# A transformer block with ALiBi attention: first norm before the weights' biases, diagonal bias added by 64-column matmuls

## The chip, the core and the metric

One NeuronCore of one Trainium2 chip runs one program: a recurrent mixer, a feed-forward layer, an attention layer, and the same feed-forward layer again. The metric is the device time of one execution in microseconds, the median of three runs. The change touches the attention layer alone.

## The reference, cut to what matters

Shapes: x is 8 × 1024 × 256 (batch, tokens, channels), 16 heads of 16 channels, all in float32.

```python
def _L0_attn_b_ref(x, Wqkv, bqkv, Wout, bout):
    qkv = (x @ Wqkv + bqkv).reshape(B, L, 3, n_heads, head_dim)
    q, k, v = (qkv[:, :, 0], qkv[:, :, 1], qkv[:, :, 2])
    scores = jnp.einsum('bqhd,bkhd->bhqk', q, k) / math.sqrt(head_dim)
    bias = -jnp.abs(pos[None, :] - pos[:, None])
    scores = scores + slopes[None, :, None, None] * bias[None, None]
    probs = jax.nn.softmax(scores, axis=-1)
    out = jnp.einsum('bhqk,bkhd->bqhd', probs, v).reshape(B, L, D)
    return out @ Wout + bout

x = x + attn_a(layernorm(x)); x = x + ffn(layernorm(x))
x = x + _L0_attn_b_ref(_layernorm(x), ...); x = x + ffn(layernorm(x))
```

The term `slopes * -|q - k|` is the one that the diagonal blocks of the change belong to.

## The kernel before, in words

**Tiling.** `attention` works through 32 groups g (8 batches × 4 groups of 4 heads). Queries and keys of a head lie in "stacks" of 64 rows (`q_stack`, `k_stack`): 48 rows of q and k split into a high and a low part, 14 rows that carry the ALiBi bias as products, and 2 rows with the row maxima as a shift. Two heads stand above one another in the 128 partitions, so a score matmul uses one half of TensorE's rows (rows 0 to 63, or 64 to 127), and two of them can run side by side.

**Two score passes.** `find_maxima` makes scores with queries in the partitions (L1588: stationary q, moving 512 keys), and VectorE takes the row maxima from PSUM (L1807). The maxima go through DRAM into the shift rows. `attend` makes the scores again with keys in the partitions (L1649: stationary k, moving 512 queries), ScalarE takes exp of two heads at once (L1758, 1024 columns), and `weigh` multiplies with v (L1604, 128×17 stationary, 256 columns, accumulated in one PSUM bank, which ScalarE copies out at L1727).

**Diagonal blocks.** Bias rows cannot express |q - k| inside a 128×128 block on the diagonal: they have one sign there. `add_block_bias` (L1532) adds what is missing to the 128 columns of that block, with two bf16 matmuls (parts): stationary is `halves[rows, part]`, a 64×128 slice of the identity, moving is `tables[rows, ..., variant, part]`, 64×128. Each part fills half of the output's partitions and adds zeros to the other half. A score tile of 512 columns has such a block when its key half and its query half are the same ("here").

**Steps.** A step here is one value of (t, pair): two L1649 (one for each half of the rows), two row turns of `find_maxima` for a group ahead (two L1588), the blocks that either has, and eight records of L1604. There are 32 × 2 × 8 × 2 = 1024 such steps. Column scores have a block in 512 of them. Row turns alternate between a pair with a block and one without. The lead before the first step does 80 of the 2048 row turns, with the second stack and the first batch's values beside them.

**Order.** Every engine runs the same generators in the same order (`schedule`, `side_by_side`): for each g the steps, with the projections of a later group (`make_stacks`), a batch's values and its norm spread between. PSUM: two pairs of banks for column scores, one for the weighed values, three in a ring (`misc`) for everything else, the row turns included.

**Start of the layer.** SyncE issues in order: identity, x of batch 0, w_out, b_v, b_qk, scale_qk, b_out, w_qk, w_v, x of batch 1. GpSimd issues the casting loads: k_bias (to DRAM), the constant rows of both stacks, halves, tables. All loads from SyncE but x and the identity count on one semaphore, `weights_in`. VectorE waits for the whole count, widens b_v (L1848) and scales b_qk (L1849); TensorE makes b_v·Wout (L1667, L1668); VectorE adds it to b_out (L1851). ScalarE and GpSimd wait for that (`bias_made`) before the schedule begins. Only then comes the norm of batch 0: stats (L1778) on VectorE, L1861 to L1872 on GpSimd, transposes (L1546), then the first projection, whose high and low parts SyncE copies into the stacks by 28 small DMAs, then the first row turn.

## Time and profile before

| | us |
|---|---|
| median of three runs | 3480.31 (3478.15 to 3480.33) |
| the profiled execution | 3481.96 |
| its span, first to last instruction | 3480.2 |
| attention's start: first load issued to first row turn | 1157.4 to 1224.5 |
| lead: first row turn to first L1649 | 1224.5 to 1291.9 |
| steps: first to last L1649 | 1291.9 to 3098.2 |

```profile
PE 3223.5 (93%) x31396; PEld 1914.4 (55%) x31396; DVE 2473.6 (71%) x4742; ACT 1998.0 (57%) x2999; POOL 768.7 (22%) x888
PE   7999999967999389999999999999999999978998
PEclk8999999978999669999999999999999999999999
```

The first line is each engine's busy time over the whole span, PE being TensorE's matmuls and PEld its weight loads. The other two are the span in 40 equal slices of 87 us: PE's busy share in tenths, and the granted TensorE clock in tenths of full speed. The layer begins at the slice with the 3; its steps are the run of nines with a clock of 9 (which stands for 90% or more) behind it. A matmul's record covers its way through the array too, so records overlap, and a busy PE is no measure of how many columns it takes in.

### The profile page before, as it was taken

The page shows a single profiled execution, that of the slowest core. Times are in us where ns is not written, and L with a number is a line of the kernel's source. Part 1 is how long each engine was busy: PE and PEld are TensorE (multiplying, and loading weights), DVE is VectorE, ACT ScalarE, POOL GpSimd, SP SyncE. Part 2 cuts the span into 40 slices and gives each one's busy share as a digit, 9 for nine tenths or more (in the row PEclk, how much of TensorE's full clock was granted, in tenths as well). Part 3 has the DMA queues.
Part 4 walks back from the last instruction along what each step waited for, and adds up shares of the span by engine and source line. Part 5 has one row for each costly group of instructions (what it writes and reads, how often), then busy time and mean ns, then how long its engine had stood idle before and what let it go on. Part 6 is the DMA issues. An engine that isn't in the chain of part 4 may idle for free. (4 is left out here: it accounts for less than half of the span.)

```text
span 3480.2 us, 77977 instructions
## 1 busy us (share of the span) xinstructions
PE 3223.5 (93%) x31396; PEld 1914.4 (55%) x31396; DVE 2473.6 (71%) x4742; ACT 1998.0 (57%) x2999; POOL 768.7 (22%) x888
## 2 busy tenths in 40 slices
PE   7999999967999389999999999999999999978998
PEld 3666666655777244444444444444444444437777
DVE  6777777737777168767778677677786776817776
ACT  3444444524555117666667666666676666765555
POOL 3445444422222201011020020110201201011222
PEclk8999999978999669999999999999999999999999
DMA  1000000012111412121222131212221312111110
GB/s 51 14 26 27 26 26 26 14 49 70 49 49 43 92 34 44 27 53 36 44 47 44 23 68 29 57 31 43 47 45 24 68 30 49 24 41 61 55 54 33
DMA packets 110295, 145.49 MB, mean 42 GB/s; under 512 B 21616, under 2 KB 94208, under 8 KB 109152
## 3 DMA queue, kind: packets, MB, share of 16 engines
q1 hardware_dynamic: 109168, 137.69, 16.8%
q8 instruction: 249, 4.08, 0.5%
q0 software_dynamic: 768, 2.82, 0.4%
q14 instruction: 110, 0.90, 0.1%
HBM read 53.89 MB, written 38.24 MB: 26 GB/s over the span
## 5 line engine op out<-in xcount | busy, mean ns | idle before, releaser
L1807 DVE TENSOR_REDUCE b_half_max<-banks 128x1 f32<-128x512 f32 x2048 | 1314.3, 685 | 441.4 <-PE banks L1532 263.1
L1758 ACT ACTIVATE b_p_t<-banks 128x1024 f32<-128x1024 f32 x1024 | 1045.8, 1024 | 398.2 <-PE banks L1532 256.6
L1588 PE MATMUL banks<-b_k_stack,b_q_stack 62*128 62x512 f32 x2048 | 826.4, 475 | 34.6 <-issue 17.8
L1649 PE MATMUL banks<-b_q_stack,b_k_stack 64*128 64x512 f32 x2048 | 851.6, 469 | 0.0
L1604 PE MATMUL banks<-b_p_t,b_v 128*17 128x256 f32 x8192 | 640.9, 385 | 25.1 <-ACT b_pv L1727 24.5
L1649 PEld LDWEIGHTS banks<-b_q_stack,b_k_stack 64*128 64x128 f32 x2048 | 342.9, 185 | 432.3 <-issue 416.8
L1532 PE MATMUL banks<-b_tables,b_halves 64*128 64x128 bf16 x4096 | 435.8, 223 | 0.0
L1588 PEld LDWEIGHTS banks<-b_k_stack,b_q_stack 62*128 62x128 f32 x2048 | 336.4, 187 | 67.9 <-issue 24.6
L1137 ACT ACTIVATE ffn_relu<-banks,ffn_scale_fc 128x512 f32<-128x512 f32 x256 | 176.0, 687 | 234.2 <-PE banks L1069 234.2
L1082 PE MATMUL banks<-ffn_proj_t,ffn_r_hi 128*128 128x256 f32 x1024 | 262.0, 289 | 8.8 <-DVE ffn_r_lo L1263 8.8
L1604 PEld LDWEIGHTS banks<-b_p_t,b_v 128*17 128x17 f32 x8192 | 135.9, 95 | 225.3 <-issue 77.3
L1083 PE MATMUL banks<-ffn_proj_t,ffn_r_lo 128*128 128x256 f32 x1024 | 253.2, 280 | 0.0
L1532 PEld LDWEIGHTS banks<-b_tables,b_halves 64*128 64x128 bf16 x4096 | 185.0, 96 | 117.1 <-issue 57.3
L1261 DVE CAST ffn_r_hi<-ffn_square 128x512 fp32r<-128x512 f32 x256 | 128.8, 503 | 142.3 <-ACT ffn_square L1141 140.8
L1889 POOL TENSOR_TENSOR b_qk_lo<-b_qk,b_qk_hi 128x512 fp32r<-128x512 f32 x64 | 81.7, 1276 | 655.4 <-ACT b_qk L1707 498.0
L1082 PEld LDWEIGHTS banks<-ffn_proj_t,ffn_r_hi 128*128 128x128 f32 x1024 | 194.4, 190 | 24.3 <-DVE ffn_r_lo L1263 14.9
L1065 PE MATMUL banks<-ffn_x_hi,ffn_fc_t 128*128 128x512 f32 x512 | 203.4, 397 | 0.0
L1066 PE MATMUL banks<-ffn_x_lo,ffn_fc_t 128*128 128x512 f32 x512 | 202.9, 396 | 0.0
L1083 PEld LDWEIGHTS banks<-ffn_proj_t,ffn_r_lo 128*128 128x128 f32 x1024 | 193.4, 189 | 8.2
L1319 POOL TENSOR_TENSOR ffn_x<-ffn_x,ffn_scaled_out 128x256 f32<-128x256 f32 x128 | 107.9, 843 | 402.6 <-DVE ffn_scaled_out L1274 402.6
L1263 DVE TENSOR_TENSOR ffn_r_lo<-ffn_square,ffn_r_hi 128x512 fp32r<-128x512 f32 x256 | 177.2, 692 | 8.8
L1141 ACT ACTIVATE ffn_square<-ffn_relu 128x512 f32<-128x512 f32 x256 | 161.8, 632 | 8.1
(232 smaller groups left out, 4728.1 us busy)
## 6 DMA issues: line engine op xcount, KB each, us to landing
ffn_x<-x SPq DMA_DIRECT2D x32, 512.0 KB, 3.8
b_q_stack<-b_qk_hi SPq DMA_DIRECT2D x256, 64.0 KB
b_k_stack<-b_qk_hi SPq DMA_DIRECT2D x256, 64.0 KB
a_x<-hidden_states SPq DMA_DIRECT2D x16, 512.0 KB, 4.3
x<-a_x SPq DMA_DIRECT2D x16, 512.0 KB, 2.9
x<-ffn_x SPq DMA_DIRECT2D x16, 512.0 KB, 2.8
b_x<-x SPq DMA_DIRECT2D x8, 1024.0 KB, 6.2
b_k_stack<-b_qk_lo SPq DMA_DIRECT2D x128, 64.0 KB
```

Of the source, the lines that this page charges most:

```text
L1065: pe.matmul(b, fc_t[:, kt, cols], x_hi[:, kt, :], start=kt == 0, stop=False)
L1066: pe.matmul(b, fc_t[:, kt, cols], x_lo[:, kt, :], start=False, stop=False)
L1082: pe.matmul(b[:, 0:DIM], r_hi[par][:, m, i * P:(i + 1) * P], proj_t[:, m, :], start=m == 0, stop=False)
L1083: last = pe.matmul(b[:, 0:DIM], r_lo[par][:, m, i * P:(i + 1) * P], proj_t[:, m, :], start=False, stop=m == HT - 1)
L1137: act.activation(relu[use % 2][:, :], high[use % 3], ACT.Relu, scale=scale_fc[:, m:m + 1]).then_inc(relu_made, 1)
L1263: dve.tensor_tensor(r_lo[par][:, m, :], square[use % 2][:, :], r_hi[par][:, m, :].bitcast(F32), ALU.subtract).then_inc(r_lo_made, 1)
L1532: last = pe.matmul(out, halves[rows, part, :], tables[rows, g % GROUPS * PAIRS + pair, variant, part, :], start=False, stop=part == PARTS ...
L1588: last = pe.matmul(m, q_stack[rows, slot, qb * P:(qb + 1) * P], k_stack[rows, slot, half * BANK:(half + 1) * BANK], start=True, stop=not h ...
L1604: last = pe.matmul(values[i * SLOT:i * SLOT + VW, cols], v[:, kb, hg * GROUP + i, :], p_t[(2 * t + i % 2) % P_BUFS][:, i // 2, cols], star ...
L1649: last = pe.matmul(out, k_stack[stack, slot, kb * P:(kb + 1) * P], q_stack[stack, slot, half * BANK:(half + 1) * BANK], start=True, stop=n ...
L1758: act.activation(p_t[use % P_BUFS][:, :, :], scores[use % 2], ACT.Exp, scale=slopes()[pair][0]).then_inc(p_made, 1)
L1807: dve.tensor_reduce(half_max[:, (pair + rg * PAIRS) * QB + qb, half:half + 1], misc.at["max", g, turn], axis=AX.X, op=ALU.max, negate=True ...
```

## The change

The identity becomes one 64×64 unit matrix for each half of the partitions (`unit`), and it is the moving operand; the table is stationary, taken with the other `variant`, since it now comes out transposed. Each part writes 64 of the block's 128 columns, in all 128 partitions. The number of matmuls and of weight loads stays.

At the start, the weights count on three semaphores (qk, v, out), and w_qk is loaded first. Nothing waits for all of them: b_qk is scaled behind the first stats, b_v is widened with the first values, b_v·Wout is made by TensorE behind the eighth tile of the first values, and GpSimd waits for the sum at its first use. GpSimd's loads wait until x of batch 0 has landed; unit and tables are issued behind the seventh and eighth normalized tile.

```diff
--- before.py
+++ after.py
@@ -82,7 +82,7 @@
     by_head = power[:, :, :, None, None] * short
     c["c_block"] = by_head.reshape(GROUPS, ROWGROUPS, GROUP // ROWGROUPS, 2, P // STACK, STACK, P).transpose(
         1, 5, 0, 2, 3, 4, 6).reshape(P, HEADS // ROWGROUPS, 2, P // STACK, P)
-    c["c_halves"] = np.tile(np.eye(P).reshape(P // STACK, STACK, P).transpose(1, 0, 2), (ROWGROUPS, 1, 1))
+    c["c_unit"] = np.tile(np.eye(STACK), (ROWGROUPS, 1))
@@ -1392,7 +1392,7 @@
         PARTS = P // STACK
         WIDTH = BANK // 2
 
-        ident, halves = sb("ident", [P, P]), sb("halves", [P, PARTS, P], BF16)
+        ident, unit = sb("ident", [P, P]), sb("unit", [P, STACK], BF16)
         tables = sb("tables", [P, HEADS // ROWGROUPS, 2, PARTS, P], BF16)
@@ -1427,7 +1427,8 @@
 
 
         x_in_sem, x_out_sem = [sem(f"x_in{i}") for i in range(X_BUFS)], [sem(f"x_out{i}") for i in range(X_BUFS)]
-        ident_in, weights_in, bias_cast, tables_cast = sem("ident_in"), sem("weights_in"), sem("bias_cast"), sem("tables_cast")
+        ident_in, qk_weights_in, v_weights_in, out_weights_in = sem("ident_in"), sem("qk_weights_in"), sem("v_weights_in"), sem("out_weights_in")
+        bias_cast, tables_cast, scaled = sem("bias_cast"), sem("tables_cast"), sem("scaled")
         half_set, cleared, widened = sem("half_set"), sem("cleared"), sem("widened")
         bias_ready, bias_made = sem("bias_ready"), sem("bias_made")
@@ -1446,7 +1447,7 @@
         att_turned, att_t_made = sem("att_turned"), sem("att_t_made")
         y_ready, y_made, y_added, y_biased = sem("y_ready"), sem("y_made"), sem("y_added"), sem("y_biased")
 
-        WEIGHTS, TABLES = 5 + GROUPS + KT, 2 * ROWGROUPS + 2
+        QK_WEIGHTS, OUT_WEIGHTS, TABLES = GROUPS + 2, KT + 2, 2 * ROWGROUPS + 2
         misc = Ring([banks[:, i, :] for i in (5, 6, 7)], (cleared, 1))
         STEPS, STACKS, VALUES, NORMALIZE = GROUP * HALVES * QB, 2, QB, 1 + QB
 
@@ -1527,9 +1528,11 @@
 
         def tensor(pe):
             def add_block_bias(out, g, pair, rg, variant):
+
                 rows = slice(rg * STACK, (rg + 1) * STACK)
                 for part in range(PARTS):
-                    last = pe.matmul(out, halves[rows, part, :], tables[rows, g % GROUPS * PAIRS + pair, variant, part, :],
+                    cols = slice(part * STACK, (part + 1) * STACK)
+                    last = pe.matmul(out[:, cols], tables[rows, g % GROUPS * PAIRS + pair, 1 - variant, part, :], unit[rows, :],
                                      start=False, stop=part == PARTS - 1, tile_position=(rg * STACK, 0))
                 return last
 
@@ -1547,19 +1550,34 @@
                     last.then_inc(xn_turned, 1)
                     yield
 
+            def bias_of_values():
+
+                m, (used, n) = misc.take(("bias",), (bias_made, 1))
+                pe.wait_ge(used, n)
+                pe.wait_ge(out_weights_in, 16 * OUT_WEIGHTS)
+                pe.wait_ge(widened, 1)
+                pe.matmul(m[:, 0:DIM], b_v_wide[:, 0, :], w_out[:, 0, :], start=True, stop=False)
+                pe.matmul(m[:, 0:DIM], b_v_wide[:, 1, :], w_out[:, 1, :], start=False, stop=True).then_inc(bias_ready, 1)
+
             def make_values(b):
                 xn_t = xn_ts[b % 2]
+                if b == 0:
+                    pe.wait_ge(v_weights_in, 16)
                 pe.wait_ge(xn_t_made, 4 * (b + 1))
                 for i in range(QB):
                     m, (used, n) = misc.take(("v", b, i), (v_made, QB * b + i + 1))
                     pe.wait_ge(used, n)
                     pe.matmul(m[:, 0:DIM], xn_t[:, 0, i * P:(i + 1) * P], w_v[:, 0, :], start=True, stop=False)
                     pe.matmul(m[:, 0:DIM], xn_t[:, 1, i * P:(i + 1) * P], w_v[:, 1, :], start=False, stop=True).then_inc(v_ready, 1)
+                    if (b, i) == (0, QB - 1):
+                        bias_of_values()
                     yield
 
             def make_stacks(g):
                 b, hg = divmod(g, GROUPS)
                 xn_t = xn_ts[b % 2]
+                if g == 0:
+                    pe.wait_ge(qk_weights_in, 16 * QK_WEIGHTS)
                 pe.wait_ge(xn_t_made, 4 * (b + 1))
                 for half in range(HALVES):
                     cols = slice(half * BANK, (half + 1) * BANK)
@@ -1661,11 +1679,6 @@
             follow, finish_tails = tails(weigh, conclude)
             pe.wait_ge(ident_in, 16)
             pe.wait_ge(cleared, 1)
-            pe.wait_ge(weights_in, 16 * WEIGHTS)
-            m, _ = misc.take(("bias",), (bias_made, 1))
-            pe.wait_ge(widened, 1)
-            pe.matmul(m[:, 0:DIM], b_v_wide[:, 0, :], w_out[:, 0, :], start=True, stop=False)
-            pe.matmul(m[:, 0:DIM], b_v_wide[:, 1, :], w_out[:, 1, :], start=False, stop=True).then_inc(bias_ready, 1)
             schedule(attend, find_maxima, make_stacks, make_values, normalize, row_parts=2)
             finish_tails()
 
@@ -1698,6 +1711,8 @@
                     use, cols = 2 * g + half, slice(half * BANK, (half + 1) * BANK)
                     m = misc.at["qk", g, half]
                     act.wait_ge(qk_ready, use + 1)
+                    if use == 0:
+                        act.wait_ge(scaled, 1)
                     if g:
                         for i in range(GROUP):
                             act.wait_ge(stacked[slot_of(g - 1) + i], 112 * ((g - 1) // SETS + 1))
@@ -1764,7 +1779,6 @@
             follow, finish_tails = tails(weigh, conclude)
             act.wait_ge(ident_in, 16)
             act.wait_ge(cleared, 1)
-            act.wait_ge(bias_made, 1)
             schedule(attend, find_maxima, make_stacks, make_values, normalize)
             finish_tails()
 
@@ -1781,11 +1795,20 @@
                 for i in range(QB):
                     last = dve.bn_aggr(mean_var[:, i, :], stats[:, i, :])
                 last.then_inc(moments, 1)
+                if b == 0:
+                    dve.wait_ge(qk_weights_in, 16 * QK_WEIGHTS)
+                    dve.tensor_scalar(b_scaled[:, :], b_qk[:, :], scale_qk[:, 0:1], None, ALU.mult).then_inc(scaled, 1)
                 for _ in range(NORMALIZE):
                     yield
 
             def make_values(b):
-                for _ in range(VALUES):
+                if b == 0:
+                    dve.wait_ge(out_weights_in, 16 * OUT_WEIGHTS)
+                    dve.tensor_copy(b_v_wide[:, :, :], spread(b_v[:, :], P)).then_inc(widened, 1)
+                for i in range(VALUES):
+                    if (b, i) == (0, VALUES - 1):
+                        dve.wait_ge(bias_ready, 1)
+                        dve.tensor_tensor(b_out[:, :], b_out[:, :], misc.at["bias",][:, 0:DIM], ALU.add).then_inc(bias_made, 1)
                     yield
 
             def make_stacks(g):
@@ -1844,11 +1867,6 @@
             dve.memset(values, 0.0).then_inc(cleared, 1)
             dve.wait_ge(ident_in, 16)
             dve.wait_ge(cleared, 1)
-            dve.wait_ge(weights_in, 16 * WEIGHTS)
-            dve.tensor_copy(b_v_wide[:, :, :], spread(b_v[:, :], P)).then_inc(widened, 1)
-            dve.tensor_scalar(b_scaled[:, :], b_qk[:, :], scale_qk[:, 0:1], None, ALU.mult)
-            dve.wait_ge(bias_ready, 1)
-            dve.tensor_tensor(b_out[:, :], b_out[:, :], misc.at["bias",][:, 0:DIM], ALU.add).then_inc(bias_made, 1)
             schedule(attend, find_maxima, make_stacks, make_values, normalize)
             finish_tails()
 
@@ -1871,6 +1889,9 @@
                     for j in range(2):
                         pool.tensor_scalar(xn[j][:, :], x[:, i + j, :], minus_mean[:, i + j:i + j + 1], norm_rstd[:, i + j:i + j + 1],
                                            ALU.add, ALU.mult).then_inc(xn_made, 1)
+                    if (b, i) == (0, QB - 2):
+                        pool.dma_start(unit[:, :], d["c_unit"]).then_inc(tables_cast, 16)
+                        pool.dma_start(tables[:, :, :, :, :], d["c_block"]).then_inc(tables_cast, 16)
                     yield
                     yield
 
@@ -1911,6 +1932,8 @@
                     pool.wait_ge(y_made, tile + 1)
                     pool.tensor_tensor(x, x, y[tile % 2][:, :], ALU.add).then_inc(y_added, 1)
                     pool.wait_ge(y_added, tile + 1)
+                    if tile == 0:
+                        pool.wait_ge(bias_made, 1)
                     pool.tensor_tensor(x, x, b_out[:, :], ALU.add).then_inc(y_biased, 1)
                     yield
 
@@ -1924,14 +1947,12 @@
             follow, finish_tails = tails(weigh, conclude)
             pool.memset(minus_half[:, :], -0.5).then_inc(half_set, 1)
             every_slot = lambda ap: ap.unsqueeze(1).to_broadcast([ap.shape[0], SETS * PAIRS, SEQ])
+            pool.wait_ge(x_in_sem[0], 16)
             pool.dma_start(k_bias, d["c_kbias"]).then_inc(bias_cast, 16)
             for first in range(0, P, STACK):
                 pool.dma_start(q_stack[first + MAIN:first + SHIFTROW, :, :], every_slot(d["c_qrows"])).then_inc(tables_cast, 16)
                 pool.dma_start(k_stack[first + SHIFTROW:first + STACK, :, :], every_slot(d["c_krows"])).then_inc(tables_cast, 16)
-            pool.dma_start(halves[:, :, :], d["c_halves"]).then_inc(tables_cast, 16)
-            pool.dma_start(tables[:, :, :, :, :], d["c_block"]).then_inc(tables_cast, 16)
             pool.wait_ge(half_set, 1)
-            pool.wait_ge(bias_made, 1)
             schedule(attend, find_maxima, make_stacks, make_values, normalize)
             finish_tails()
 
@@ -2010,15 +2031,15 @@
             follow, finish_tails = tails(weigh, conclude)
             sp.dma_start(ident[:, :], d["c_ident"]).then_inc(ident_in, 16)
             load(0)
-            sp.dma_start(w_out[:, :, :], tiled(d["Wout"])).then_inc(weights_in, 16)
+            sp.dma_start(w_qk[:, :, :, :].rearrange("p k g n -> p k (g n)"), tiled(d["Wqkv"][:, 0:2 * DIM])).then_inc(qk_weights_in, 16)
+            sp.dma_start(scale_qk[:, :], d["c_qkscale"]).then_inc(qk_weights_in, 16)
+            for g in range(GROUPS):
+                sp.dma_start(b_qk[:, g:g + 1], column(d["bqkv"][g * P:(g + 1) * P])).then_inc(qk_weights_in, 16)
+            sp.dma_start(w_v[:, :, :], tiled(d["Wqkv"][:, 2 * DIM:3 * DIM])).then_inc(v_weights_in, 16)
+            sp.dma_start(w_out[:, :, :], tiled(d["Wout"])).then_inc(out_weights_in, 16)
             for kt in range(KT):
-                sp.dma_start(b_v[:, kt:kt + 1], column(d["bqkv"][2 * DIM + kt * P:2 * DIM + (kt + 1) * P])).then_inc(weights_in, 16)
-            for g in range(GROUPS):
-                sp.dma_start(b_qk[:, g:g + 1], column(d["bqkv"][g * P:(g + 1) * P])).then_inc(weights_in, 16)
-            sp.dma_start(scale_qk[:, :], d["c_qkscale"]).then_inc(weights_in, 16)
-            sp.dma_start(b_out[:, :], d["bout"].partition_broadcast(P)).then_inc(weights_in, 16)
-            sp.dma_start(w_qk[:, :, :, :].rearrange("p k g n -> p k (g n)"), tiled(d["Wqkv"][:, 0:2 * DIM])).then_inc(weights_in, 16)
-            sp.dma_start(w_v[:, :, :], tiled(d["Wqkv"][:, 2 * DIM:3 * DIM])).then_inc(weights_in, 16)
+                sp.dma_start(b_v[:, kt:kt + 1], column(d["bqkv"][2 * DIM + kt * P:2 * DIM + (kt + 1) * P])).then_inc(out_weights_in, 16)
+            sp.dma_start(b_out[:, :], d["bout"].partition_broadcast(P)).then_inc(out_weights_in, 16)
             load(1)
             schedule(attend, find_maxima, make_stacks, make_values, normalize)
             finish_tails()
```

## Rows read from the trace of the kernel before

**Rows 1.** Costliest groups (xcount | busy, mean ns of one | idle before, releaser)

```profile
L1807 DVE TENSOR_REDUCE b_half_max<-banks 128x1 f32<-128x512 f32 x2048 | 1314.3, 685 | 441.4 <-PE banks L1532 263.1
L1532 PE MATMUL banks<-b_tables,b_halves 64*128 64x128 bf16 x4096 | 435.8, 223 | 0.0
```

**Rows 2.** Three stretches: length, busy us of each engine, then PEclk, DMA share, GB/s

```profile
1157.00:1224.40 67.40, 12.96 (x28) 5.92 (x28) 4.93 (x22) 5.28 (x8) 13.37 (x21) 0.53 0.55 113
1224.40:1292.00 67.60, 62.88 (x203) 31.49 (x203) 48.54 (x80) 6.42 (x14) 2.98 (x3) 0.65 0.19 34
1310.00:3103.00 1793.00, 1744.11 (x17287) 851.01 (x17284) 1321.90 (x2223) 1225.35 (x1455) 216.28 (x279) 1.00 0.21 40
```

**Rows 3.** Timeline of TensorE, two steps: start us, us, what

```profile
1600.78 0.50 PE L1649 MATMUL banks<-b_q_stack,b_k_stack 64*128 64x512 f32 x1
...
1602.01 0.50 PE L1649 MATMUL banks<-b_q_stack,b_k_stack 64*128 64x512 f32 x1
...
1602.35 0.28 PE L1532 MATMUL banks<-b_tables,b_halves 64*128 64x128 bf16 x2
...
1603.40 0.50 PE L1649 MATMUL banks<-b_q_stack,b_k_stack 64*128 64x512 f32 x1
```

**Rows 4.** The same view, two steps with blocks in the column scores

```profile
1623.16 0.50 PE L1649 MATMUL banks<-b_q_stack,b_k_stack 64*128 64x512 f32 x1
...
1624.56 0.50 PE L1649 MATMUL banks<-b_q_stack,b_k_stack 64*128 64x512 f32 x1
...
1624.90 0.29 PE L1532 MATMUL banks<-b_tables,b_halves 64*128 64x128 bf16 x4
...
1625.31 0.29 PE L1532 MATMUL banks<-b_tables,b_halves 64*128 64x128 bf16 x4
1625.54 0.63 PE L1604 MATMUL banks<-b_p_t,b_v 128*17 128x256 f32 x8
1626.09 0.50 PE L1649 MATMUL banks<-b_q_stack,b_k_stack 64*128 64x512 f32 x1
```

**Rows 5.** Timeline of the weight loads in the step at 1602.01

```profile
1602.34 0.11 PEld L1532 LDWEIGHTS banks<-b_tables,b_halves 64*128 64x128 bf16 x2
1602.41 0.19 PEld L1649 LDWEIGHTS banks<-b_q_stack,b_k_stack 64*128 64x128 f32 x1
```

**Rows 6.** Matmuls of the mixer with 64 and 32 moving columns, by form

```profile
L341 PE MATMUL banks<-a_q_up,a_k_up 32*64 32x32 f32 x4480 | 83.9, 217 | 0.0
L341 PE MATMUL banks<-a_q,a_k 32*64 32x64 f32 x896 | 38.9, 244 | 0.0
```

**Rows 7.** Waits, 1292 to 3103: us in total, times, longest

```profile
PEld banks L1604 <- ACT b_pv L1727: 37.7, 63, 1.0
```

**Rows 8.** Timeline of all engines at the layer's start

```profile
1157.80 0.60 SPq L1944 DMA_DIRECT2D b_x<-x  x1
1157.92 0.80 POOL L1927 DMA_DIRECT2D b_k_bias<-c_kbias  x1 [0.42 <-issue]
...
1160.99 0.61 POOL L1931 DMA_DIRECT2D b_halves<-c_halves  x1
...
1183.15 0.29 DVE L1848 COPY b_b_v_wide<-b_b_v 128x256 f32<-128x256 f32 x1 [24.59 <-DMA b_w_v<-Wqkv]
...
1186.01 2.71 DVE L1778 BATCH_NORM_STATS2 b_stats<-b_x 128x6 f32<-128x256 f32 x8
...
1189.60 0.25 POOL L1861 TENSOR_SCALAR b_norm_rstd<-b_mean_var 128x8 f32<-128x8 f32 x1 [27.44 <-DVE b_mean_var L1782]
...
1224.47 0.89 PE L1588 MATMUL banks<-b_k_stack,b_q_stack 62*128 62x512 f32 x2 [17.82 <-issue]
```

**Rows 9.** Loads issued in 1157 to 1170: KB each, median us to landing

```profile
b_x<-x SPq DMA_DIRECT2D x1, 1024.0 KB, 16.5
...
b_tables<-c_block POOLq DMA_DIRECT2D x1, 1024.0 KB, 18.5
b_k_bias<-c_kbias POOLq DMA_DIRECT2D x1, 896.0 KB, 7.7
```

**Rows 10.** Landing of x, all eight batches

```profile
DMA to landing us min/median/max: 4.4/5.6/16.5
```

## The prediction

> **What bounds the kernel now.** I first read the costliest groups. The row maxima on VectorE cost 1314 us and the diagonal matmuls 436 us of records, so both could bound the layer [rows 1]. The stretches decide it: while the steps run (1310 to 3103), PE is busy 97% at full clock, VectorE 74%, ScalarE 68% [rows 2]. Records overlap, so I then read the timeline of TensorE, step by step, and there the bound is plain. A step without blocks takes 1.23 us from one L1649 to the next, one with blocks in the row turns 1.39 us [rows 3], one with blocks in the column scores 1.40 us, and one with both 1.53 us [rows 4]. The same work always takes the same time, so these steps wait for no other engine; the blocks cost 0.17 us alone and 0.30 together. The start has another bound: from 1157.8 to 1183.15 the engines wait for loads, then b_v·Wout takes until 1186.0, and only there does the norm begin [rows 8]. The lead (67.6 us) has 80 reductions in 48.5 us of VectorE beside 62.9 us of PE at mean clock 0.65: the two take turns [rows 2].
>
> **Part 1: diagonal matmuls of 64 columns.** Number of matmuls and loads: unchanged. Per matmul: 128 columns at the granted full clock of 2.4 GHz are 53 ns, 64 are 27, so at most 27 ns go. How much of it is on the path?
> - In a row-turn step, the order on one half of the array is: scores, part 0, part 1, load of the next stationary (L1649), its 512 columns. That load starts at 1602.41, 0.07 us after the blocks' first load, that is as part 1 starts, and takes 0.19 [rows 5]; part 1's columns run beside it. So only part 0 stands on the path: 27 ns. The step's second block lies on the other half, whose scores were already under way; it ends before the scores of the first half do. It costs nothing now and gives nothing.
> - A column-score step is the mirror of it: 27 ns.
> - In a step with both, both halves have a block twice. The first pair (1624.90) again gives part 0 only. The second pair (1625.31) is the last thing before L1604 at 1625.54 [rows 4], with no load to hide in; there both parts count, 54 ns. Together 81 ns.
>
> Counts: column blocks are in 512 of 1024 steps; row turns made during steps are 2048 − 80 = 1968, so 984 pairs, 492 with a block, half of these (246) beside a column block. That is 246 with both, 246 with row blocks only, 266 with column blocks only: 246 × 81 + 512 × 27 ns = 19.9 + 13.8 = 33.7 us. The lead comes below. Taken off: in 63 steps the first L1604 of a new sum waits for ScalarE's copy L1727 (37.7 us in all, 0.6 each) [rows 7]; that chain starts at the L1604 before, so what TensorE does meanwhile is covered. I take 45 ns a step as lost, 63 × 45 ns = 2.8 us. Part 1 gives 31 us.
>
> Bounds: no row shows a bf16 matmul of 64 columns. Nearest are the mixer's records, 244 ns with 64 fp32 columns and 217 with 32, 27 ns apart [rows 6]: a narrower moving operand does shorten a matmul at this size. The pair of diagonal loads lasts 0.11 us where one lasts about 0.10 [rows 5], so loads can follow one another some 15 ns apart, less than 27. From above: if all four or eight 27 ns of a step counted, 246 × 216 + 512 × 108 ns = 108 us; the layout of the step rules most of this out, and I take 36 us as upper end. From below: 0, if something other than columns sets the pace. I stay at 31, nearest to the step rows. VectorE does not take over: after the change the mean step is (1.23 + 1.36 + 1.37 + 1.45)/4 = 1.35 us with two reductions, whose starts can lie 0.61 us apart (48.5 us for 80), 1.21 us. Exp is one of 1.02 us a step.
>
> The Trainium skill speaks against this part: "TensorE: Matmul & The Clock Gate", LDWEIGHTS (loading the stationary operand), prices a load by its columns at 1.2 GHz, an estimate of 107 ns for these 128; under the next heading it calls some bf16 loads faster. A pair bound by such loads would gain nothing from fewer columns and part 1 would be 0. The two loads above lie far closer, and I follow them.
>
> **Part 2: the start.** The loads of x of batch 0 took 16.5 us to land (1157.8 to 1174.3) [rows 8, 9], against 5.6 in the median of all eight batches [rows 10], because GpSimd's casting loads ran beside them. With these held back, x lands at about 1163.4. VectorE starts the stats there instead of at 1186.01: 22.5 us earlier. What follows is the same chain, 38.4 us from the stats (1186.01) to the first row turn (1224.47) [rows 8]. What could break it:
> - GpSimd now first issues its five remaining loads, 1157.92 to 1160.99 in the old run, 3.1 us [rows 8]. Its first op of the norm came 3.6 us behind the stats' start. So they just fit. If descriptors keep GpSimd longer, the bound is the landing of k_bias, 7.7 us [rows 9]: 4 us late. Zero is my value, since the old issues go on at 0.6 us each.
> - w_qk and its companions are needed 14 us after the stats, at 1178. They stand right behind x in SyncE's queue. Before, everything had landed by 1183.15; if that held, 5 us would go. I take 0.
> - k_bias is needed by SyncE's first stack copy 23.6 us behind the stats; there is room. tables is issued near 1176 behind the seventh and eighth tile. Even with the 18.5 us of before [rows 9] it lands at 1195, and the first row turn is due at 1202. unit and tables cost GpSimd two issues of 0.6 behind the last tiles, with only qk_lo far behind them.
> - b_v·Wout moves into the lead: 1183.15 to 1186.01, 2.9 us for widening, four matmuls and the addition [rows 8]. The matmuls and their bank count on TensorE, while VectorE's own parts fit its idle time. Price −2.2, bounds 0 and 2.9.
>
> x landing late is bounded by 16.5 us: then 11.7 us are left of the 22.5. The lead's clock changes between its two levels (0.65 in the mean), and a lead that begins 22 us earlier meets other moments: ±4 us, taken as 0. Part 2 gives 20.3 us.
>
> **Sum.** 31 + 20.3 = 51.3. The lead has 40 turns with a block; part 0 is 53 ns shorter at 1.2 GHz, 2.1 us, of which I count a third, since VectorE sets the pace of the rest: 0.7. Together 52. The profiled execution took 3481.96 (span 3480.2 and 1.8 around it): 3430. It stood 1.65 us above the median: 3428.
>
> **Rivals.**
> - *The narrow matmuls don't get faster* (load of 128 columns, or a floor per instruction). For it: nothing of this form is in the trace, and the mixer's loads of 64 fp32 columns keep its 32-column matmuls from coming at 27 ns. Against it: the loads 15 ns apart. Only the start is left: 3460. Chance 0.11.
> - *The start gives a third.* x lands late, or GpSimd is held by descriptors, whose writing no row here shows. 8 instead of 20 us: 3440. Chance 0.14. The Trainium skill, "DMA: Bandwidth & Descriptors", SWDGE vs HWDGE vs iDMA, has GpSimd's own cores write the descriptors of such loads. No run here shows what an operation behind them waits; the norm's operations are now behind five of them.
> - *The clock falls inside the steps*, the slower side. TensorE gets less to do in each step, and in the lead, with PE busy 93% by its records, the clock was at the lower level for much of the time (0.65) [rows 2]. At 1.2 GHz the array's work takes about twice as long, so a step of 1.35 us becomes some 2.3. Each 100 us spent at half clock then lose 41 (1 − 1.35/2.3), so about 125 us of them eat all 52, and with 200 us it would be 3428 + 82 = 3510. Against it: the steps ran 1793 us at 1.00 without one fall, the stretches where TensorE waits for ScalarE among them [rows 2, 7]. Chance 0.03.
> - *The change doesn't do what it says*: a late wait (tables, scaled) keeps the start as it was and the blocks gain nothing, 3480. Chance 0.03.
>
> The forecast has 0.69, with its own range 3419 to 3438. The range 3414 to 3450 takes in the second rival and the bounds of both parts, and leaves out the first, the clock and the no-change case. Less than 0.2% (7 us) can't be told from no change here. Faster 0.94, same 0.03, slower 0.03.
>
> **What would show it.** Right: steps of 1.23, 1.37, 1.37 and 1.45 us; L1532's successor about 27 ns shorter per record; stats starting near 1163.5, first row turn near 1202, first L1649 near 1271; clock 1.00 throughout the steps. Wrong: unchanged step lengths with shorter records (loads or issue bind), stats started but GpSimd's first norm op more than 4 us behind them, a wait for tables before the first row turn, or half clock after 1310.

## The result, and the profile after

| | before | after |
|---|---|---|
| median of four runs, us | 3479.51 (3478.15 to 3480.33) | 3434.52 (3431.39 to 3438.02) |
| the profiled execution | 3481.96 | 3436.67 |
| x of batch 0 issued to stats | 28.2 | 6.2 |
| stats to first row turn | 38.5 | 38.3 |
| lead, to the first column scores | 67.5 | 72.0 |
| steps, first to last column scores | 1806.3 | 1777.2 |
| last column scores to the end | 382.0 | 383.4 |

The ratio is 0.9871, 95% interval 0.9854 to 0.9888: faster by 45 us, 6.5 us short of the 3428 forecast and inside its range. The two profiled executions differ by 45.3 us of span, and the table splits it: start −22.2, lead +4.5, steps −29.1, rest +1.4.

The costliest groups show what became narrower and what did not. A block's matmul record is 26 ns shorter than in [rows 1] (223 to 197), VectorE's reductions are as long as they were, and the loads keep 96 ns in a record of their own.

```profile
L1830 DVE TENSOR_REDUCE b_half_max<-banks 128x1 f32<-128x512 f32 x2048 | 1311.1, 686 | 413.5 <-PE banks L1535 241.5
...
L1535 PE MATMUL banks<-b_unit,b_tables 64*128 64x64 bf16 x4096 | 372.0, 197 | 0.0
...
L1535 PEld LDWEIGHTS banks<-b_unit,b_tables 64*128 64x128 bf16 x4096 | 185.0, 96 | 120.5 <-issue 76.6
```

The stretches answer to [rows 2], with the same columns (start, lead, steps). The layer's start is 45 us instead of 67, the steps still run at clock 1.00, and the lead has the same 48.7 us of reductions, but its clock is 0.56 where it was 0.65.

```profile
1157.00:1202.20 45.20, 10.73 (x24) 4.68 (x24) 4.29 (x20) 5.28 (x8) 13.40 (x21) 0.54 0.79 167
1202.20:1274.30 72.10, 67.60 (x205) 34.26 (x206) 48.66 (x81) 6.42 (x14) 2.99 (x3) 0.56 0.18 32
1310.00:3056.00 1746.00, 1694.11 (x17111) 836.95 (x17110) 1302.43 (x2196) 1213.11 (x1441) 215.47 (x278) 1.00 0.21 41
```

TensorE's timeline answers to [rows 4]: a step with column blocks begins at 1600.94, one with both at 1602.31. From one first L1667 to the next they take 1.37 and 1.46 us, where they took 1.40 and 1.53.

```profile
1600.94 0.50 PE L1667 MATMUL banks<-b_q_stack,b_k_stack 64*128 64x512 f32 x1
...
1602.31 0.50 PE L1667 MATMUL banks<-b_q_stack,b_k_stack 64*128 64x512 f32 x1
...
1602.66 0.23 PE L1535 MATMUL banks<-b_unit,b_tables 64*128 64x64 bf16 x4
...
1603.05 0.24 PE L1535 MATMUL banks<-b_unit,b_tables 64*128 64x64 bf16 x4
1603.21 0.63 PE L1622 MATMUL banks<-b_p_t,b_v 128*17 128x256 f32 x8
1603.77 0.50 PE L1667 MATMUL banks<-b_q_stack,b_k_stack 64*128 64x512 f32 x1
```

The timeline of all engines at the start answers to [rows 8]. x is issued at 1157.87 and the stats begin 6.2 us later, behind nothing but x. GpSimd issues its loads only then, and its first norm operation (L1879) begins right as the moments are there, 0.30 us idle before it.

```profile
1157.87 0.62 SPq L1965 DMA_DIRECT2D b_x<-x  x1
...
1164.02 2.71 DVE L1792 BATCH_NORM_STATS2 b_stats<-b_x 128x6 f32<-128x256 f32 x8 [5.39 <-DMA b_x<-x]
1164.19 0.79 POOL L1951 DMA_DIRECT2D b_k_bias<-c_kbias  x1 [6.62 <-DMA b_x<-x]
...
1166.73 0.56 POOL L1954 DMA_DIRECT2D b_k_stack<-c_krows  x1
...
1167.59 0.25 POOL L1879 TENSOR_SCALAR b_norm_rstd<-b_mean_var 128x8 f32<-128x8 f32 x1 [0.30 <-DVE b_mean_var L1796]
...
1177.45 0.55 POOL L1894 DMA_DIRECT2D b_tables<-c_block  x1
```

The landings of what is issued in this stretch answer to [rows 9]: tables take 8.7 us where they took 18.5.

```profile
b_tables<-c_block POOLq DMA_DIRECT2D x1, 1024.0 KB, 8.7
b_k_bias<-c_kbias POOLq DMA_DIRECT2D x1, 896.0 KB, 9.7
...
b_w_qk<-Wqkv SPq DMA_DIRECT2D x1, 512.0 KB, 6.2
```

### The profile page after: what moved, and what is told of

Read it like the earlier page. It is cut to its first block and busy times, and to the rows that moved or that the text cites. A ratio compares the mean times of both kernels' runs of the same rounds, so it can differ in the third digit from the quotient of the medians.

```text
span 3434.9 us, 77978 instructions
## 1 busy us (share of the span) xinstructions
PE 3194.9 (93%) x31396; PEld 1909.6 (56%) x31396; DVE 2471.0 (72%) x4742; ACT 2001.2 (58%) x2999; POOL 770.2 (22%) x888
## 5 line engine op out<-in xcount | busy, mean ns | idle before, releaser
L1667 PE MATMUL banks<-b_q_stack,b_k_stack 64*128 64x512 f32 x2048 | 839.6, 469 | 0.2 <-DMA b_q_stack<-b_shift_dram 0.2
L1622 PE MATMUL banks<-b_p_t,b_v 128*17 128x256 f32 x8192 | 640.9, 385 | 27.2 <-ACT b_pv L1742 26.7
L1667 PEld LDWEIGHTS banks<-b_q_stack,b_k_stack 64*128 64x128 f32 x2048 | 343.0, 185 | 433.2 <-issue 410.4
L1535 PE MATMUL banks<-b_unit,b_tables 64*128 64x64 bf16 x4096 | 372.0, 197 | 0.0
L1535 PEld LDWEIGHTS banks<-b_unit,b_tables 64*128 64x128 bf16 x4096 | 185.0, 96 | 120.5 <-issue 76.6
L1622 PEld LDWEIGHTS banks<-b_p_t,b_v 128*17 128x17 f32 x8192 | 135.9, 95 | 199.1 <-ACT b_p_t L1773 59.3
L1082 PEld LDWEIGHTS banks<-ffn_proj_t,ffn_r_hi 128*128 128x128 f32 x1024 | 194.5, 190 | 24.6 <-DVE ffn_r_lo L1263 15.1
```

The lines of the kernel that those rows point to most:

```text
L1082: pe.matmul(b[:, 0:DIM], r_hi[par][:, m, i * P:(i + 1) * P], proj_t[:, m, :], start=m == 0, stop=False)
L1535: last = pe.matmul(out[:, cols], tables[rows, g % GROUPS * PAIRS + pair, 1 - variant, part, :], unit[rows, :], start=False, stop=part == P ...
L1622: last = pe.matmul(values[i * SLOT:i * SLOT + VW, cols], v[:, kb, hg * GROUP + i, :], p_t[(2 * t + i % 2) % P_BUFS][:, i // 2, cols], star ...
L1667: last = pe.matmul(out, k_stack[stack, slot, kb * P:(kb + 1) * P], q_stack[stack, slot, half * BANK:(half + 1) * BANK], start=True, stop=n ...
```

## The experiments

How they are read. The layer before attention ends at another time in each execution (x was issued anywhere from 1151 to 1169 us), with identical code. So beside the ratio of whole runs I give, from each kernel's profiled execution, the time from the issue of x to the last column scores ("layer"), its parts, and the medians of the steps by kind (none, row block, column block, both), taken over the steps without projections or other extra work. Before and after have

| | x to stats | lead | steps | layer | step: none / row / column / both, ns |
|---|---|---|---|---|---|
| before | 28.2 | 67.5 | 1806.3 | 1940.4 | 1224 / 1400 / 1396 / 1530 |
| after | 6.2 | 72.0 | 1777.2 | 1893.6 | 1224 / 1374 / 1375 / 1453 |

### Either half of the change alone, and the whole again

`start_alone` has the new start with the old blocks; `mm_alone` has the old start with the new blocks:

```diff
-    last = pe.matmul(out, halves[rows, part, :], tables[rows, ..., variant, part, :], ...)
+    last = pe.matmul(out[:, cols], tables[rows, ..., 1 - variant, part, :], unit[rows, :], ...)
```

> The kernel after with the diagonal blocks as before (identity slices stationary, tables moving, 128 columns). If the two parts add up as in the changed kernel's trace (start 22.2 us earlier, a lead some 2 to 5 us longer, steps 29.1 us shorter), this one is 17 to 22 us faster than the kernel before, steps of 1.40 and 1.53 us stay. Rival: the longer lead (72.0 against 67.5 us) comes from the narrow matmuls, which leave TensorE with less to do; then the lead here is 67 to 70 us and the gain 20 to 22.

> The kernel before with the diagonal blocks of the change (table stationary, 64 columns moving), its start untouched. Theory: steps of 1.37, 1.37 and 1.45 us, first to last column score 29 us shorter (1777 us), the first row turn at 1224.5 as before; 28 to 30 us faster. Rival (narrow matmuls lengthen the lead): lead 70 to 72 us, gain only 25.

`after_again` is the changed kernel once more, on the same chip as these.

> The changed kernel itself, for the size of both parts together and for a second trace of its lead. Its runs so far fell on 3431 to 3432 and 3437 to 3438 us. If the clock of the lead makes that difference, the lead (first row turn to first column score) will differ from 72.0 us by what the total differs, with another share of half clock in it, and the steps will be 1777 us again. Total: 44 to 50 us faster than before.

| | ratio, 95% | x to stats | lead (of it at half clock) | steps | layer |
|---|---|---|---|---|---|
| start_alone | 0.995 (0.9932 to 0.9968) | 6.2 | 68.7 (46.1) | 1807.3 | 1920.6 |
| mm_alone | 0.9913 (0.989 to 0.9935) | 28.0 | 70.9 (64.1) | 1776.5 | 1913.7 |
| after_again | 0.9859 (0.9836 to 0.9881) | 6.0 | 70.7 (60.4) | 1776.2 | 1890.9 |

The parts do not meet. The start alone gives 19.8 us of the layer and leaves the steps alone; the matmuls alone give 26.7 and leave the start alone; the sum, 46.5, is what both do together (46.8, again 49.5). The traced execution of `after_again` took 3442.35 us, 5.7 more than the first one of the same kernel, with a lead 1.3 shorter: that difference lies ahead of attention (x issued 6.8 us later), not in the lead's clock as I had supposed.

The lead went as the two rivals had it, not as the theories: 68.7 us with the start alone (rival 67 to 70), 70.9 with the matmuls alone (rival 70 to 72, and a gain of 25 in place of 28 to 30). So it lengthened by 3.4 us with the matmuls and by 1.2 with the start. The windows over the two leads (length, busy us of PE, PEld, VectorE, ScalarE, GpSimd, then the granted clock) show the same VectorE work and another clock; first `start_alone`:

```profile
1207.00:1275.70 68.70, 63.84 (x205) 32.34 (x206) 48.83 (x81) 6.41 (x14) 3.00 (x3) 0.66 0.19 33
```

and `mm_alone`:

```profile
1221.80:1292.70 70.90, 66.58 (x201) 33.32 (x202) 48.25 (x80) 6.43 (x14) 2.99 (x3) 0.55 0.19 32
```

### Is it the hold or the order of the loads?

`no_hold` leaves GpSimd's first five casting loads (k_bias and the stacks' constant rows) where they were in time, beside x, and keeps everything else of the change, the late issue of unit and tables too.

```diff
-            pool.wait_ge(x_in_sem[0], 16)
             pool.dma_start(k_bias, d["c_kbias"]).then_inc(bias_cast, 16)
```

> The kernel after without GpSimd's wait for x of batch 0, so its casting loads start at 1158 beside x and the weights. Theory: contention delays x as before (landing 16.5 us after issue), the stats start near 1174 instead of 1164 and the first row turn near 1212: 8 to 10 us slower than the changed kernel. Rival (the order of SyncE's loads alone brings x in early): x lands within 7 us, the same time as the changed kernel.

Ratio 0.9884 (0.9864 to 0.9903), layer 1904.4, 10.8 us above the changed kernel; the rival, that the order of SyncE's loads does it, fell. x takes 16.3 us to land, nearly as before the change (16.5 [rows 9]), and the stats begin 16.4 us after its issue. The timeline of its start:

```profile
1151.74 0.62 SPq L1964 DMA_DIRECT2D b_x<-x  x1
1151.86 0.79 POOL L1950 DMA_DIRECT2D b_k_bias<-c_kbias  x1 [0.42 <-issue]
...
1168.12 2.71 DVE L1792 BATCH_NORM_STATS2 b_stats<-b_x 128x6 f32<-128x256 f32 x8 [15.61 <-DMA b_x<-x]
```

So the start's 22 us are two things: 11.8 from stats that wait for nothing but x, neither for the weights nor for b_v·Wout (28.2 to 16.4), and 10.2 from keeping five of GpSimd's loads away from x (16.4 to 6.2). Holding back tables, 1 MB more, did next to nothing for x by itself: x landed 16.3 us after its issue without that load beside it, 16.5 with it.

### Is it the 64 columns, or the swapped operands?

`swap_wide` swaps the operands as the change does but keeps 128 moving columns, half of them zeros, written into the whole block. `third_part` keeps 64 columns and adds a third, zero, part.

```diff
# swap_wide
-    last = pe.matmul(out[:, cols], tables[rows, ..., 1 - variant, part, :], unit[rows, :], ...)
+    last = pe.matmul(out, tables[rows, ..., 1 - variant, part, :], halves[rows, part, :], ...)
# third_part
-    for part in range(PARTS):
+    for n, part in enumerate((0, 1, 1)):
...
+        moving = unit[rows, STACK:] if n == 2 else unit[rows, 0:STACK]
```

> The kernel after with the table stationary but 128 columns moving: a 64x128 slice of the identity, each part fills half of the block's columns and adds zeros to the other half. It tells the swap of the operands from the width. Theory (columns alone): steps 1.40, 1.40 and 1.53 us as before the change, total as the start alone, 3460 us. Rival (the swap itself helps, since the same kind of operand streams): steps as after, 3434 us.

> The kernel after with a third matmul in every diagonal block: same stationary as part 1, 64 columns of zeros moving, so zeros are added. Theory: every part but the last of a block stands on the path when a load of a score stationary follows, and all of them when the weighing follows; one more costs 29 ns in a step with one block kind and 58 ns in a step with both. Steps 1.40, 1.40 and 1.51 us, total 25 to 30 us slower than the changed kernel. Rival (a floor per instruction sets the pace and width doesn't matter): 56 and 112 ns, total 55 us slower.

| | ratio, 95% | lead (half clock) | steps | step: none / row / column / both, ns |
|---|---|---|---|---|
| swap_wide | 0.9938 (0.992 to 0.9957) | 71.6 (58.6) | 1804.9 | 1224 / 1400 / 1396 / 1530 |
| third_part | 0.9949 (0.9928 to 0.9971) | 71.2 (58.7) | 1807.8 | 1225 / 1434 / 1405 / 1508 |

With wide columns every kind of step is what it was before to the nanosecond, so the swap is worth nothing and the columns are worth all of it. Its group has the old length of a record too:

```profile
L1534 PE MATMUL banks<-b_halves,b_tables 64*128 64x128 bf16 x4096 | 436.1, 223 | 0.0
```

The third part cost 30 ns in a column step, which is a narrow matmul's own spacing (in a run of them both starts and ends of the records lie 29 ns apart), 55 in a step with both, and 60 in a row step, where the forecast had 29: twice what the columns explain. TensorE's timeline of such a row step shows why:

```profile
1627.80 0.49 PE L1668 MATMUL banks<-b_q_stack,b_k_stack 64*128 64x512 f32 x1
1627.80 0.49 PE L1607 MATMUL banks<-b_k_stack,b_q_stack 62*128 62x512 f32 x1
1628.14 0.20 PE L1536 MATMUL banks<-b_unit,b_tables 64*128 64x64 bf16 x1
1628.14 0.49 PE L1607 MATMUL banks<-b_k_stack,b_q_stack 62*128 62x512 f32 x1
...
1628.23 0.47 PE L1668 MATMUL banks<-b_q_stack,b_k_stack 64*128 64x512 f32 x1
```

and that of its loads:

```profile
1628.14 0.18 PEld L1607 LDWEIGHTS banks<-b_k_stack,b_q_stack 62*128 62x128 f32 x1
```

The second row turn's load starts only at 1628.14, 0.34 us into the step. In the changed kernel that load begins about 0.11 us into the step, beside the first scores, and joins the one before it in a record of two; here is its row step's start:

```profile
1625.52 0.29 PEld L1606 LDWEIGHTS banks<-b_k_stack,b_q_stack 62*128 62x128 f32 x2
1625.86 0.11 PEld L1535 LDWEIGHTS banks<-b_unit,b_tables 64*128 64x128 bf16 x2
```

In program order the two matmuls of a row block with their loads, and the second column scores with its load, stand between the two row turns: six instructions in the changed kernel, eight in `third_part`. The load was pulled ahead past six and not past eight. It did not wait for its bank: over the 115 plain row steps VectorE's reduction had set that bank free 0.04 us into the step in both kernels, while the load began at 0.11 and at 0.34 (medians). In column steps it is the load of the second column scores that has to pass the column block, four instructions or six; it was pulled ahead in both, and the part cost its 30 ns. So blocks between two scores can cost more than their columns: they can stop the next load from hiding. By these two kernels the limit lies between six and eight; that it is a count of instructions wasn't tried in any other way.

### Blocks issued behind the scores

From this comes a version. `deferred` collects a step's blocks and issues them behind its four score matmuls (in the lead behind both row turns of a pair; always ahead of every other use of the ring), so nothing stands between the two scores of a half.

```diff
-        add_block_bias(out[:, at:at + P], g, pair, rg, int(kb < CT)).then_inc(col_scores, 1)
+        waiting_blocks.append(((out[:, at:at + P], g, pair, rg, int(kb < CT)), col_scores))
...
+        flush()     # behind the second row turn of a pair, and behind the last column scores of a step
```

> The kernel after with the blocks of a step issued behind its four score matmuls instead of behind each. Theory: the second score matmuls' stationaries (0.19 us records, about 0.1 us of it exposed behind a block) are then loaded while the first ones stream, as in the step without blocks, and the blocks stand together before the weighing: 1.22 + 2 parts (60 ns) + about 15 = 1.30 us with one kind, 1.22 + 4 parts (120) + 15 = 1.36 with both. Steps 246 x 0.09 + 512 x 0.07 = 58 us shorter, total 3377. Rival: maxima and exp start later, VectorE (1.21 us for two reductions) or a PSUM bank of the ring takes over and most of the gain is lost: 3410 to 3440.

`deferred_columns` defers the column blocks alone.

> The kernel after with only the column scores' blocks issued behind the four score matmuls; the row turns' blocks stay behind their scores. Theory (the gain of deferring is the hidden load of the next stationary, its loss the later maxima): steps without blocks stay at 1.22 us, since maxima are as early as in the changed kernel; column-block steps go from 1.37 to 1.30; steps with both stay near 1.45, because the half with the first row block still has an exposed load. 266 x 0.07 = 19 us faster than the changed kernel. Rival (steps without blocks grew in the deferred kernel for another reason than late maxima): they are 1.26 us here too.

| | ratio, 95% | lead | steps | layer | step: none / row / column / both, ns |
|---|---|---|---|---|---|
| deferred | 0.98 (0.9778 to 0.9823) | 74.9 | 1750.9 | 1868.9 | 1260 / 1299 / 1302 / 1360 |
| deferred_columns | 0.98 (0.9775 to 0.9825) | 70.8 | 1762.1 | 1876.4 | 1224 / 1374 / 1298 / 1454 |

Steps with one kind of block fall by some 75 ns, three times what 64 columns gave, steps with both by 93. Deferring columns alone changes column steps alone.

The step lengths came as forecast, the sum did not: I had 58 us for the steps and 3377 in all; measured were 26.3 and 3414.85, in the range of the rival. Against the changed kernel, the 248 steps with row blocks gave 16.0 us and the 244 with both 13.4. The 267 with column blocks gave 6.3 in place of 19, because the 76 of them with extra work became 3.6 us longer, and the 264 without blocks took 9.5 back. `deferred_columns` gave 15.1 us of the 19 forecast (median 3416.49). The timeline of a `deferred` step with both blocks shows all eight block matmuls in one run behind the scores, and the step is 1.36 us long:

```profile
1604.40 0.50 PE L1679 MATMUL banks<-b_q_stack,b_k_stack 64*128 64x512 f32 x1
1604.40 0.73 PE L1616 MATMUL banks<-b_k_stack,b_q_stack 62*128 62x512 f32 x2
1604.75 0.40 PE L1679 MATMUL banks<-b_q_stack,b_k_stack 64*128 64x512 f32 x1
1604.98 0.29 PE L1545 MATMUL banks<-b_unit,b_tables 64*128 64x64 bf16 x8
1605.20 0.63 PE L1634 MATMUL banks<-b_p_t,b_v 128*17 128x256 f32 x8
1605.76 0.49 PE L1679 MATMUL banks<-b_q_stack,b_k_stack 64*128 64x512 f32 x1
```

One thing is given back: a step without blocks goes from 1224 to 1260 ns in the median. In such a step, begun at 1623.70 behind one with row blocks, the second row turn's load stands 0.30 us into the step instead of 0.11:

```profile
1623.70 0.18 PEld L1616 LDWEIGHTS banks<-b_k_stack,b_q_stack 62*128 62x128 f32 x1
1623.81 0.19 PEld L1679 LDWEIGHTS banks<-b_q_stack,b_k_stack 64*128 64x128 f32 x1
1624.00 0.18 PEld L1616 LDWEIGHTS banks<-b_k_stack,b_q_stack 62*128 62x128 f32 x1
```

and VectorE is in the reduction that frees this turn's bank, which belonged to the turn three before it, until 1623.94:

```profile
1623.25 0.69 DVE L1843 TENSOR_REDUCE b_half_max<-banks 128x1 f32<-128x512 f32 x1 [0.24 <-PE banks L1545]
```

My reading was that its bank is not free yet: the blocks of the step before end later, so do the maxima. `deferred_steps` tests a remedy, row blocks ahead of column blocks in the run, and in the lead, where VectorE waits for each turn, no deferral. `deferred_again` repeats `deferred` beside it.

```diff
+        waiting_blocks.sort(key=lambda waiting: waiting[1] is col_scores)
...
-        if turn % 2:
+        if turn % 2 or STEPS * g + turn < STEPS + LEAD:
             flush()
```

> The deferred kernel with two edits: in the lead a row block follows its scores at once, as in the changed kernel, and in a step the row turns' blocks are issued ahead of the column scores'. Theory (deferring costs where maxima come late and the ring's bank is not free): lead 71 to 72.5 us instead of 74.9, steps with both still 1.36 us, steps without blocks between 1.22 and 1.26, as the maxima of a step with both start 60 ns earlier while those of a row-block step don't; 3 to 8 us faster than the deferred kernel, near 3405. Rival (VectorE's rate, not the moment of its start, holds the steps without blocks): steps sum as in the deferred kernel, 1751 us, and only the lead gains.

> The deferred kernel once more, beside the last one on the same chip: steps 1751 us, lead near 75, 68 to 74 us faster than the kernel before.

| | median, us | ratio, 95% | lead (half clock) | steps | step: none / row / column / both, ns |
|---|---|---|---|---|---|
| deferred_steps | 3407.28 | 0.9787 (0.9768 to 0.9807) | 70.6 (59.3) | 1752.5 | 1258 / 1300 / 1301 / 1360 |
| deferred_again | 3408.42 | 0.9789 (0.9768 to 0.9809) | 76.0 (70.0) | 1752.3 | 1266 / 1300 / 1302 / 1359 |

The order of blocks changed nothing in these medians, so my remedy fell. The reading stands all the same, and the traces show it once the steps are sorted by the kind of step before them:

| step without blocks | bank free at | load starts at | step takes |
|---|---|---|---|
| changed kernel, behind a row step (102) | −0.07 | 0.11 | 1.224 |
| deferred, behind a step without blocks (17) | 0.16 | 0.21 | 1.220 |
| deferred, behind a row step (102) | 0.24 | 0.30 | 1.277 |
| deferred_steps, behind a row step (102) | 0.24 | 0.29 | 1.277 |

"Bank free" is the end of that reduction; all times are medians in us from the step's start. In `deferred` the load starts 0.05 us behind it in steps with column blocks and with row blocks too; the exception are the 23 steps with both that follow a row step. A row step has no column blocks, so putting row blocks ahead of them moves nothing there: the remedy could not reach the steps that lose. A load at 0.21 costs nothing and one at 0.30 costs 53 ns.

The lead is 4 to 5 us shorter, but with less of it at half clock, so this can't be put down to the order alone. In whole runs the two versions can't be told apart. They stand 76 and 75 us under the kernel before, the first run of `deferred` 67; for the changed kernel it was 45 and 47. The two kernels were not run side by side, and 20 to 30 us between them is what this gives.

### Can the lead be had at full clock?

`warm_lead` puts 60 full-array matmuls of the identity ahead of the first row turn, and one ahead of each turn of the lead; they write a bank that the first column scores overwrite.

```diff
+                warm(60)
...
+                    if STEPS * g + turn < STEPS + LEAD:
+                        warm(1)
```

> The kernel after with extra matmuls that compute nothing that is used (identity times identity, 128 columns, into a score bank that the first step overwrites): 60 before the first row turn, while TensorE waits for the stack copies, and one before each of the 80 row turns of the lead. Theory (the lead is 72 us since it runs 60 to 64 us of them at half clock): the granted clock is full in most of the lead, VectorE sets its pace (80 reductions at 0.61 us, 49 us, and some idle time for the values), lead 55 to 60 us, total 12 to 17 us faster than the changed kernel. Rival (the clock stays at half, or the lead is bound by VectorE and PSUM banks at either clock): the extra matmuls cost 0.2 to 0.4 us a turn, lead 75 to 95 us, total slower than the changed kernel.

Ratio 0.9984 (0.9967 to 1.0002): the whole gain of the change was lost, and the lead came out above both ranges. The traced execution (3463.78 us) is the fastest of ten whose median is 3480.57, so in most others the loss was larger than this trace shows. The first window is the whole lead, the others a piece at mostly full and one at mostly half clock (length, busy us with counts of PE, PEld, VectorE, ScalarE, GpSimd, clock, DMA, GB/s):

```profile
1197.10:1303.70 106.60, 106.60 (x364) 64.94 (x366) 55.46 (x82) 6.39 (x14) 2.98 (x3) 0.73 0.13 22
1200.00:1240.00 40.00, 40.00 (x150) 23.96 (x151) 22.52 (x34) 4.04 (x7) 2.54 (x2) 0.86 0.17 29
1280.00:1310.00 30.00, 30.00 (x97) 17.56 (x96) 13.89 (x21) 3.24 (x6) 0.45 (x1) 0.56 0.01 3
```

The clock did rise to 0.73, and the lead took 106.6 us. A turn took 0.84 to 0.92 us in the fast piece and 1.45 to 1.58 in the slow one, against some 0.60 for a turn of the changed kernel's lead without other work between. So a filler in each turn costs 0.25 to 0.3 us even at full clock, and the filler, not the clock, set the pace. Most of that is the filler itself. The 60 in a row came 0.22 us apart at full clock (1180 to 1186); in the lead the loads of filler and row turn follow each other by 0.42 us each, none beside the other:

```profile
1226.40 0.30 PEld L1592 LDWEIGHTS banks<-b_ident 128*128 128x128 f32 x2 [0.24 <-issue]
1226.82 0.18 PEld L1613 LDWEIGHTS banks<-b_k_stack,b_q_stack 62*128 62x128 f32 x1
1227.24 0.30 PEld L1592 LDWEIGHTS banks<-b_ident 128*128 128x128 f32 x2 [0.24 <-issue]
```

What half-array matmuls lose by standing between full ones was not separated from the filler's own length, and cheaper fillers were not tried. The fillers did not hold the clock up either: from 1256 to 1300 it was at its lower level again.

## Why the prediction was right, point by point

**The block matmuls.** Forecast: steps of 1.23, 1.37, 1.37, 1.45 us. Measured medians: 1.224, 1.374, 1.375, 1.453. The reading that only part 0 stands on the path of a block step, and both parts in the second pair of a step with both, was right to within 6 ns a step, and `swap_wide` shows that the columns did it. The sum was 31 us for 29.1 measured. By kind of step the savings are 5.6 us (row, 248 steps), 9.2 (column, 267), 15.2 (both, 244) and −0.9 (none, 264).

The deduction for the waits behind ScalarE's copy, 2.8 us, can be read from the traces step by step, and it was right. The wait itself stayed (37.3 us after, 37.7 before [rows 7]). In 31 groups a sum of weighed values is copied out in the fourth step, in 32 one in the twentieth. The third and fourth steps together gained 48 ns in the mean where 27 + 81 were priced: the third gained 102, and the fourth, which waits, gave 54 back. The twentieth gained nothing where 27 was priced. That is 2.7 us lost. The 1.9 us that are missing lie elsewhere and are spread: the first four steps, which run partly at half clock, fell short of their price by 0.9, steps without blocks became 0.9 longer in all, which no term of the sum had, and every other kind is within 0.5 of its price.

"The same work always takes the same time" holds for the steps that I showed, not for all. In 23 steps with both blocks TensorE waits up to 0.8 us for ScalarE's copy of the turned maxima; such a step takes 2.48 us in place of 1.53, 17.5 us of waiting in all. These steps gained as the others did (80 ns), since the wait lies ahead of the blocks.

The reason I gave for two cheap parts, part 1's columns beside the next scores' load, agrees with the loads too: in plain row steps that load starts 0.410 us into the step before and 0.382 after (medians), as part 1 starts, and the scores follow it by 27 ns in both. Part 0's 28 ns are gone from the path and part 1's were never on it. `third_part` agrees in column steps (+30) and not in row steps (+60), where another mechanism, the load that isn't pulled ahead, comes on top. So 27 ns per exposed part holds only while the count of instructions between two scores of a half stays small. The change kept this count, and I had not seen that it mattered.

**The narrow matmuls might not be faster.** Fell: the records of two narrow matmuls on one half end 29 ns apart where wide ones ended 56 apart (they start 40 and 67 apart), and the pair of loads is still 0.11 us. The load price of the Trainium skill (page "TensorE: Matmul & The Clock Gate", LDWEIGHTS, an estimate of 107 ns for 128 columns) would have made part 1 nothing; the trace sides with the loads 15 ns apart.

**The start.** Forecast: x lands 5.6 us after its issue, stats 22.5 us earlier, GpSimd's five issues just fit, chain of 38.4 us unchanged. Measured: 6.0, 22.0, 3.57 us from the stats to GpSimd's first norm operation with 0.30 idle before it, and 38.3. w_qk landed 6.2 us after its issue, tables at 8.7, and nothing waited for either. Each of these was taken from a row, and `no_hold` shows that the two halves of the start's gain are of the size that [rows 9] and the old wait for the weights gave: had x landed as late as before, the forecast of 11.7 us left was right too (measured 11.8).

**The lead.** This is the one step that missed in size: forecast +2.2 for b_v·Wout less 0.7 for the blocks, +1.5 with ±4; measured +4.5 (3.2 in the repetition). The two experiments split it. The start alone added 1.2 us, with no more of the lead at half clock than before (46.1 us for 47.0): that is b_v·Wout, priced at 2.2. The matmuls alone added 3.4 us with nothing more to do, and there 64.1 us were at half clock, 17 more; that is the part I had taken as 0 within ±4. That the clock makes these 3.4 us is argued from this, not tested by itself. Eight kernels whose lead has the same work or nearly so fall into two groups:

| | lead | at half clock |
|---|---|---|
| before | 67.5 | 47.0 |
| start_alone | 68.7 | 46.1 |
| deferred_steps | 70.6 | 59.3 |
| after_again | 70.7 | 60.4 |
| mm_alone | 70.9 | 64.1 |
| third_part | 71.2 | 58.7 |
| swap_wide | 71.6 | 58.6 |
| after | 72.0 | 63.0 |

The two with 46 to 47 us at half clock are the shortest; within the six others length and share do not go together. `swap_wide` has the new start and wide columns and yet the longer share, so narrower columns are not the cause of it by themselves. What the two short leads have in common, against the six, is the old block matmul with the table moving; two kernels don't show that this is the cause, and it stays open. The bound of ±4 us for a lead that meets the clock at another moment had the right size; the value 0 inside it was the error, and in both executions of the changed kernel it went the same way.

**The end.** From the last column scores on nothing was forecast; it took 1.4 us more, with 3.4 us from 3057.3 at half clock. In the other kernels this stretch lies between 381.5 and 385.5, before at 382.0; the difference is within that spread.

**The sum.** 52 forecast, 45.4 measured by the parts of the profiled executions. Of the 6.6 us between, 1.9 are missing in the steps, 0.3 at the start, 3.0 in the lead and 1.4 behind the steps. The clock rival (chance 0.03) did not come: 1.00 through all steps, although TensorE had less to do in each.

## What to carry to other kernels

Read the path step by step from the timeline, by kind of step, and price an edit only where its instructions are exposed: 4096 records each 26 ns shorter were worth 106 us on paper and 29 in time. Before narrowing small matmuls between large ones, move them behind the large ones: that gave 26 us more in the steps, nearly as much again, because the next load then hides; but look at what the later results hold up, here the reductions and with them a bank. Where a layer's first operation waits for one load, hold back what other queues would carry beside it: without GpSimd's casting loads beside x, 10 of its 16 us went.

## What the runs showed of the hardware that I had not expected

- Matmuls on different 64-row halves do not keep the order in which they are issued across halves: in a row-block step of the changed kernel the second row turn, on one half (in program order behind the second column scores, on the other), started 0.34 us into the step, the column scores 0.41.
- A weight load was pulled ahead past six instructions of such code and not past eight: it started 0.11 or 0.34 us into the step, with its bank free at 0.04 in both. The third narrow matmul cost 30 ns or 60 with it.
- bf16 matmuls of 64 columns on 64 rows ended 29 ns apart, those of 128 columns 56, with a load of 128 columns each.
- One full-array filler in each turn of half-array matmuls: 0.25 to 0.3 us a turn at full clock, of which the filler back to back takes 0.22; some 0.9 at half clock.
- x, 1 MB, landed in 6.0 us beside the weights on its own queue, and in 16.3 with five casting loads of GpSimd there too.
